# A recurrent block and a cross-attention block on one core: from one loop with both interleaved to three stages

## What is computed

```python
# layer 0, per sequence
xa = _ln(x); sx = shifted(xa) - xa
t = tanh((xa + sx * maa_x) @ maa_w1); m_j = t_j @ maa_w2        # five mixes j = w k v r g
x_j = xa + sx * (maa_j + m_j)
w = exp(-exp(time_decay + tanh(xw @ decay_w1) @ decay_w2))
r = xr @ Wr.T; k = xk @ Wk.T; v = xv @ Wv.T; g = silu(xg @ Wg.T)
# 32 heads of 16: per token   out = r . (faaaa * k v + s);  s = k v + w * s
x = x + (group_norm(out) * g) @ Wo.T
xc = _ln(x); ...; x = x + sigmoid(xr2 @ fWr.T) * (square(relu(xk2 @ fWk.T)) @ fWv.T)
# layer 1, latents = x, 16 heads of 32, keys and values from context and latents (487 rows)
q = latents @ q_w + q_b; k, v = concat(ctx, latents) @ kv_w + kv_b
attn = softmax(mask(q k / 32)); o = attn v @ out_w + out_b + latents
out = gelu(rmsnorm(o) @ mlp_w1 + mlp_b1) @ mlp_w2 + mlp_b2 + latents
```

## Time and profile before

| what | value |
|---|---|
| median of three runs | 1222.49 us |
| the profiled execution's own time | 1224.26 us |
| its span | 1222.2 us |
| mean granted clock of TensorE | 0.911 |
| first turn (no attention in it) | 0 to 151 us |
| seven turns of the loop | 151 to 1007 us, 119 to 128 us each |
| attention of the last sequence | 1007 to 1047 us |
| MLP | 1047 to 1222 us |

### The profile page before, as it was taken

How to read it: one execution, slowest core, us unless ns; L and a number is a source line. 1 busy time by engine, 2 the same in 40 slices (tenths; PEclk the granted TensorE clock), 3 DMA queues, 4 the chain that set the end, 5 groups by cost and what they waited for, 6 DMA issues and landing times.

```text
span 1222.2 us, 18100 instructions
## 1 busy us (share of the span) xinstructions
PE 1051.5 (86%) x6748; PEld 741.1 (61%) x6748; DVE 625.0 (51%) x1204; ACT 411.2 (34%) x934; POOL 270.3 (22%) x231
## 2 busy tenths in 40 slices
PE   5658998799789978997799879987998697999998
PEld 5525684368447834674477447843784364788886
DVE  2543248425952594358335842684268423644544
ACT  3112244134422442253235312442254225533332
POOL 2420143105410540144014400540053000200100
PEclk9768997899899989998899779998998895899999
DMA  7470122012201120122012201220122046000200
GB/s 286 117 225 8 33 69 67 1 48 68 66 8 40 68 66 15 33 68 66 15 33 68 66 10 38 68 66 8 40 68 66 0 182 232 1 0 0 61 0 30
DMA packets 25779, 73.23 MB, mean 60 GB/s; under 512 B 8173, under 2 KB 10093, under 8 KB 24350
## 3 DMA queue, kind: packets, MB, share of 16 engines
q1 hardware_dynamic: 25758, 72.94, 18.8%
HBM read 65.82 MB, written 7.11 MB: 60 GB/s over the span
## 4 chain that ended last, share of the span: by engine, by line
issue 41%; PE 31%; POOL 13%; DVE 7%; SPq 2%; DMA 2%; ACT 2%; POOLq 0%; DVEq 0%; ACTq 0%
POOL region L381 9%; PE bank L1241 7%; PE bank L1229 6%; PE bank L965 5%; DVE region L489 3%; PE bank L1000 3%; PE bank L972 3%; DMA region<-v_scratch 2%; PE bank L1031 2%; POOL region L384 2%; SPq L237 2%; PE bank L1015 1%; DVE region L496 1%; PE bank L1049 1%; POOL xj L374 1%
## 5 line engine op out<-in xcount | busy, mean ns | idle before, releaser
L965 PE MATMUL bank<-xj,wbig 128*128 128x112 f32 x1280 | 174.7, 302 | 29.2 <-DVE xj L533 23.8
L965 PEld LDWEIGHTS bank<-xj,wbig 128*128 128x128 f32 x1280 | 169.1, 217 | 34.2 <-DVE xj L533 25.5
L381 POOL TENSOR_TENSOR region<-region,ks 128x896 f32<-128x896 f32 x64 | 139.2, 2174 | 221.6 <-DMA region<-v_scratch 221.5
L457 DVE SCALAR_TENSOR_TENSOR tmp<-bank,vec,sx 128x112 f32<-128x112 f32 x160 | 41.7, 327 | 183.4 <-PE bank L987 181.3
L745 ACT ACTIVATE smb<-smb,nmax 112x487 f32<-112x487 f32 x128 | 88.1, 690 | 80.8 <-DVE nmax L569 80.8
L1049 PE MATMUL bank<-ident,smb 112*125 112x112 f32 (+1 forms) x512 | 88.1, 313 | 29.4 <-ACT smb L745 28.9
L496 DVE TENSOR_TENSOR region<-region,rt 128x896 f32<-128x896 f32 x64 | 105.4, 1647 | 7.4 <-ACT rt L833 1.8
L1000 PE MATMUL bank<-region,wbig 128*128 128x375 f32 x256 | 103.5, 559 | 0.0
L1015 PE MATMUL bank<-region,place 128*32 128x448 f32 x256 | 42.8, 751 | 68.7 <-DVE region L496 68.7
L1049 PEld LDWEIGHTS bank<-ident,smb 112*125 112x125 f32 (+1 forms) x512 | 66.0, 200 | 58.5 <-ACT smb L745 57.5
L569 DVE CUSTOM_DVE_ANT_0 smb<-bank,mask_b 112x487 f32<-112x487 f32 x128 | 78.1, 660 | 27.7 <-issue 27.7
(11 more groups left out here) (154 smaller groups left out, 1627.4 us busy)
## 6 DMA issues: line engine op xcount, KB each, us to landing
region<-v_scratch SPq DMA_DIRECT2D x64, 448.0 KB
wbig<-in_w SPq DMA_DIRECT2D x2, 4096.0 KB, 15.1
region<-in_ctxt SPq DMA_DIRECT2D x9, 750.0 KB, 4.6
wbig<-in_wbig SPq DMA_DIRECT2D x3, 2048.0 KB, 16.2
wbig<-in_wbig SPq DMA_DIRECT2D x3, 1024.0 KB
region<-in_wbig SPq DMA_DIRECT2D x2, 1024.0 KB, 10.9
x_in<-in_x SPq DMA_DIRECT2D x9, 224.0 KB, 2.6
v_scratch<-vt SPq DMA_DIRECT2D x32, 56.0 KB, 1.6
```

The lines of the kernel that those rows point to most:

```text
L381: g.tensor_tensor(buf, buf, ks[:, k:k + 1, 0:T].broadcast_to([P, VS, T]), ALU.mult).then_inc(s["a_ready"], 1)
L965: i = t_.matmul(tiles(dst)[:, m, :], w[:, k, m * P:(m + 1) * P], x[:, k, :], start=k == 0, stop=k == NT - 1)
```

## The change

The loop is taken apart into three stages, and all python loops over sequences are written out.

1. **Recurrent block of all sequences, a pipeline of three.** `period(i)` for i = -1 to 8 on every engine holds, interleaved in a fixed order: the scan of sequence b = i, the part behind the scan of a_ = i - 1 (group norm, Wo, channel mix), the inputs, mixes and k, v, r, g products of d = i + 1, and the last step (`latents`) of i - 2. `ks` and `gate` are double. The squares of the group norm and of the relu move from DVE to ACT. Latents go to DRAM by rows (`lat_scratch`) and by columns (`latc_scratch`).
2. **Attention of all sequences** with split products. `kv(b, n)` makes keys (n < 4) and values of all 488 rows (487 and a pad), context and latents together, in 12 fp32r products each; `query` and `output_projection` are split in three as well. `kv(b + 1, ...)` stands between the steps of `attention(b)`. ACT makes the high parts (`weight_high`, `context_high`, `attention_high`), DVE the low ones.
3. **MLP**: its 32 steps as before, its buffers elsewhere.

Each stage's buffers lie in the room of the last, in one `arena`. The core of the diff follows, engine by engine.

SP, after the stores and chunk loads of sequence 0, and at the end of stage 1:

```diff
+            def late_weights():
+                sp.dma_start(x_t[:, :], a["x"][0]).then_inc(s["xt_loaded"], 16)
...
+                        sp.dma_start(W["Wo"][p:p + HT, :, :], rows_of[j, m]).then_inc(s["wlate_loaded"], 16)
...
+                                sp.dma_start(gnv[p:p + HT, i, :], of[j, m]).then_inc(s["gnv_loaded"], 16)
+                sp.dma_start(tail[:, 1:4], a["wbig"][:, 5:8]).then_inc(s["wlate_loaded"], 16)
...
+            period(-1)
+            late_weights()
+            period(0)
+            attention_weights()
...
+            period(B)
+            wait(sp, "ffn_ready", B)
+            sp.dma_start(w1[:, :, :, :], a["w1"]).then_inc(s["w1_loaded"], 16)
+            load_context(1)
+            load_mask(0)
```

POOL, the whole of `period`:

```diff
+            def period(i):
+                a_, b, d = i - 1, i, i + 1
+                if real(d):
+                    rstd(1, d)
+                if real(b):
+                    for n in (2, 3, 4):
+                        scan_input(b, n)
+                if real(a_):
+                    rstd(2, a_)
+                if real(b):
+                    scan_input(b, 5)
+                if real(d):
+                    for j in (MIX_V, MIX_K, MIX_W):
+                        mixed(d, j)
+                if real(b):
+                    scan_input(b, 6)
+                if real(d):
+                    mixed(d, MIX_R)
+                if real(b):
+                    scan_input(b, 7)
+                if real(d):
+                    mixed(d, MIX_G)
+                    scan_input(d, 0)
+                    scan_input(d, 1)
```

ACT, in `period` and at the end of `last_period`:

```diff
+                if real(a_):
+                    deviation(a_)
+                    norm_weights(a_)
+                if real(b):
+                    gate_tanh(b)
...
+                latent_columns(a_)
+                context_high(1)
```

PE, the split products and their place between the attention's steps (groups 1 and 2 of `attention` left out):

```diff
+            def kv(b, n):
+                if n == 0:
+                    pe.wait_ge(s["cx_ready"], b + 1)
...
+                        for w, c in in_parts(parts("kw"), x):
+                            i = t_.matmul(dst[:, 0:PAD], w[:, k, n * P:(n + 1) * P], c[:, k, :],
...
+                        for w, c in in_parts(parts("vw"), x):
+                            i = t_.matmul(dst[0:KT_ROWS, :], c[:, k, r:r + KT_ROWS], w[:, k, :],
...
+            def query(b):
...
+                        for w, c in in_parts(parts("qw"), x):
+                            i = t_.matmul(tiles(7)[:, m, :], w[:, k, m * P:(m + 1) * P], c[:, k, 0:T],
...
+                scores(b, 0)
+                if more:
+                    kv(b + 1, 0)
+                probs_turned(b, 0)
+                if more:
+                    kv(b + 1, 1)
+                if b:
+                    output_projection(b - 1)
+                weighted(b, 0)
...
+                scores(b, 3)
+                if more:
+                    kv(b + 1, 6)
+                    query(b + 1)
...
+                probs_turned(b, 3)
+                if more:
+                    kv(b + 1, 7)
+                sums_turned(b)
+                weighted(b, 3)
```

More of the change, by code:

```diff
@@ new lines, in build @@
+        sx = room.take("sx", [P, NT, T])
+        t4 = room.take("t4", [P, 2, T])
+        tmp = room.take("tmp", [P, 2, NT, T])
+        xxx = tmp[:, 1]
+        xj = room.take("xj", [P, 3, NT, T])
+        dt65 = room.take("dt65", [DD + 1, T])
+        maa1 = room.take("maa1", [P, NT, NMIX * DM])
+        maa2 = room.take("maa2", [P, 2, C])
+        dec1 = room.take("dec1", [P, NT, DD])
+        dec2 = room.take("dec2", [DD + 1, C])
+        room = Room(ROOM_S, ROOM_T)
+        scan = [room.take(f"scan{i}", [P, VS, T]) for i in range(NBUF)]
@@ new lines, in build @@
+        decay = [room.take(f"decay{i}", [P, VS * T]) for i in range(2)]
+        ws = room.take("ws", [P, NT, T])
+        ks = [room.take(f"ks{i}", [P, NT, T + 1]) for i in range(2)]
+        vt = room.take("vt", [P, NT, T + 1])
+        rt = room.take("rt", [P, NT, T])
+        ruk = room.take("ruk", [P, NT, T])
+        s0 = room.take("s0", [P, NT, B, S])
+        room = Room(ROOM_T, ROOM_E)
+        x_t = room.take("x_t", [T, C])
+        x2 = room.take("x2", [T, C])
+        rows_t = room.take("rows_t", [T, C])
@@ new lines, in build @@
+        xa_t = room.take("xa_t", [P, NT, T + 1])
+        sx_t = room.take("sx_t", [P, NT, T])
+        xk = room.take("xk", [P, 2, NT, T])
+        kk = room.take("kk", [P, NT, T])
+        rr = room.take("rr", [T, C])
+        lat = room.take("lat", [T, C])
+        latc = room.take("latc", [P, NT, T])
+        y_cols = room.take("y_cols", [P, NT, T])
+        y_cen = room.take("y_cen", [P, NT, T])
+        yg = room.take("yg", [P, NT, T])
+        gstd = room.take("gstd", [P, 2, T])
+        gate = [room.take(f"gate{i}", [P, NT, T]) for i in range(2)]
@@ L210, in build, with wait, real, kv_bank @@
         s = {n: sem(n) for n in names}
+        def wait(engine, name, count):
+            if count > 0:
+                engine.wait_ge(s[name], count)
+        def real(*sequences):
+            return all(0 <= i < B for i in sequences)
+        def kv_bank(b, n):
+            return n % 2 if b == 0 else HID_BANK[n % 2]
         block = ctx.enter_context(nc.Block())
@@ new lines, in mask, with group_max @@
+            def mask(b):
+                dve.wait_ge(s[f"mask_loaded{b % 2}"], 16 * (b // 2 + 1))
+                v.tensor_scalar(mask_b[b % 2][:, T:NKEY], mask_i[b % 2][:, :], 0.0, MASKED, ALU.is_equal, ALU.mult
+                                ).then_inc(s["mask_eq"], 1)
+            def group_max(b, k, first=0, last=HG):
+                if k == 0 and first == 0:
+                    dve.wait_ge(s["mask_eq"], b + 1)
+                    dve.wait_ge(s["pad_ready"], 5)
+                dve.wait_ge(s["s_done"], b * NT + k + 1)
+                for r in range(first, last):
@@ new lines, in _, with kv_keep @@
+            for i in range(-1, B):
+                period(i)
+            def kv_keep(b, n):
+                act.wait_ge(s["kv_ready"], b * NPC + n + 1)
+                if b and n == 0:
+                    wait(act, "pvh", (b - 1) * NT)
+                src = bank[kv_bank(b, n)]
+                if n < NT:
+                    c_.activation(kt[b % 2][:, n, :], src[:, 0:NKEY], ACT.Identity,
+                                  bias=V["k_b"][:, n:n + 1]).then_inc(s["kv_kept"], 1)
+                else:
+                    c_.copy(vv[b % 2][0:KT_ROWS, n - NT, :], src[0:KT_ROWS, :]).then_inc(s["kv_kept"], 1)
@@ L924, in _ @@
+            for b in range(B):
+                attention(b)
+            act.wait_ge(s["w2_loaded"], 16)
             w2_high(0, 0)
+            attention_high(B - 1)
             def step(g, p, first=False, last=False):
```

1641 lines of the change are left out of this document (949 added, 692 removed).

## The result

Before 1226.83 us, after 1129.56 us (medians of four executions each, 1221.03 to 1233.58 and 1126.10 to 1130.95): ratio 0.920, 95% interval [0.914, 0.926]. The forecast was 1193 us with 1140 to 1256 as its range.

What follows compares the result with a forecast made beforehand. PE nearly bounds the old turn; DVE was to bound stage 1, PE stage 2. Start and period 0 to 113, middle periods and period 7 to 566, then 618, 643, attention to 1020, MLP to 1192.5: 1193 us, range 1140 to 1256.

Steps and rivals of the forecast that it cites:

- the gate's stall: Middle period: DVE's gating waits for ACT's tanh, queued behind the norm's weights; 3 us, bounds 0 and 5.
- the query at one instruction's pace: Stage 2, PE: 48 split products with 112 columns, each at half an f32 instruction's cost, 5.6 us in all.
- rival 2: Stage 2 query: split products with 112 columns cost as much as f32 ones, +45, 1238 us; chance 0.20.
- rival 3: Stage 1: DVE and POOL run almost wholly in line, a middle period of 76 us, 1258 in all; chance 0.17.
- Sum: 51 + 5 + 3 + 3.5 + 3 = 65.5, taken as 66: Middle period: DVE's work, added POOL waits, in-order stalls, seam and 0.1 us step waits; bounds 55 and 84.
- 10.6 + 5.3: DVE's attention share in the earlier turn: 16 maxima at 0.66, and smaller steps estimated at half as much.
- I take 5 more: Middle period: additional DVE waits from POOL's additions and scan inputs laid beside it; 5 us, bounds 0 and 18.
- my 6: POOL waits already in DVE's 51: products with r 4.5 us, scans about 1.5 to 2.5 per sequence.
- The seam: Between middle periods: last product with r, PE's sum, whole y, then next scan awaiting POOL's input; 3.5 us, bounds 1 and 7.
- the steps that wait for the one before: Middle period: 0.1 us between a step and one that waits for it, some 30 times; 3 us.
- Rival 4: Stage 1: periods of 60 us because POOL runs during DVE's stalls, so the two don't add; 1153 us, chance 0.18.
- 47.7 with 2 for the seam: 49.6: Stage 2, one sequence: PE's summed products 47.7 us, 2 for the seam, 49.6 in all.

Runs made afterwards that it cites:

- pool_half: Against the changed kernel, POOL multiplies only half of each chunk by the keys, leaving keys out of the other half; 1090.2 us.
- rstd_late: Against the changed kernel, POOL's small power for the first norm goes behind the multiplications of chunks 2 and 3; 1121.8 us.
- gate_first: Against the changed kernel, ACT computes the gate's tanh ahead of the group norm's weights; 1119.0 us.

## Why the prediction was wrong

- **Mechanisms.** Right: DVE sets the middle period, PE stage 2; the gate's stall (3 forecast, 3.06 measured); the query at one instruction's pace (5.6 forecast, 48 products in 5.30 measured), so rival 2 fell; DVE and POOL exclude each other without the period reaching rival 3's 76; MLP 172.5 against 173.4. PE at 1.00 in stage 2 without waiting for exps.
- **The step that failed first: "Sum: 51 + 5 + 3 + 3.5 + 3 = 65.5, taken as 66"**, measured 61.0; six of these errors are 30 of the 63 us. Its first two terms both failed. For the turn of the earlier trace rows I gave the attention 10.6 + 5.3 of DVE's 68.2 us. Its timeline shows 12.0, because the maxima follow each other more closely than they last: all 16, with their reads, are busy for 9.80. That leaves 56.2 for the recurrent block and 55 behind the two squares, not 51. Of these, 10.1 us were held already: 6.2 in the products with r, 2.4 in the scans, and 1.5 in ruk (2.60 instead of 1.07), which my 6 had left out. The maxima of that turn, and ruk in it:

```profile
397.66:516.98 119.32, 9.80 (x32) 0.94 0.15 46
```

```profile
422.12 2.60 DVE L467 SCALAR_TENSOR_TENSOR ruk<-ks,vec,rt 128x112 f32<-128x112 f32 x4
```

So "I take 5 more" for POOL was the wrong term: the pipeline holds DVE for 10.5 us, 0.4 more than that turn did (8.1 to 10.1 in six turns of the loop). pool_half and rstd_late show that the held time lies on the path, not that the change added it. The durations of all steps sum to the same (57.9 before, 57.8 after), but they follow each other more closely, and DVE is busy 53.6 us. That 51 + 5 = 56 came as near as that is luck: 4 too little and 5 too much.

- **Idle time in the period** was 7.9, not 9.5. The seam took 1.9 of its 3.5, and the steps that wait for the one before took 0.8 of their 3. Against them stand 2.2 that had no term, 1.45 of it for the Wo product. Rival 4 had the length (60 against 61.0 measured), for a reason that no run showed: it let stalls and held time overlap, and both stood in line.
- **Stage 2, "47.7 with 2 for the seam: 49.6"**, measured 46.3. PE has no seam (46.12 of 46.30 busy). The transposes were priced from one row at 1.95; from start to start four groups take 6.4, not 7.8. Scores, weighted sums and inverse sums follow each other at 1.02, 0.91 and 0.8, not at the durations 1.09, 0.98 and 0.98, 0.6 too much. The products for keys and values went the other way: 22.6 instead of 21.7, since 12 with 512 columns take 2.9 here and not the MLP's 2.77. Only the last sequence was too cheap as a whole (33, where 36.2 were measured).
- **The start, the periods 0 and 8 and the change of stages** were each 2 to 7 us too long.
- **The range.** Nearly all the terms were taken on the long side: 65.5 as 66, 5 more for POOL, 2 for a seam, 1.95 for a transpose, the late end for the fifth chunk. The bounds of one period (55 to 84) held 61, and six such periods alone could have given 66 less; yet the lower end, 1140, was taken from rival 4 alone. Errors of one sign in stages that follow each other add, and the range left no room for that.

## What to carry to other kernels

Price a dense stretch by the distance between starts of its groups, not by their durations, and put no seam into it unless an engine's row shows idle time. A path over two engines that exclude each other is shortened by laying the long instruction of one beside those that are not held; here that brought less than half of what the timeline promised, and the waits at the ring of buffers grew. Before adding waits for a second engine to a busy time, take out of it, row by row, those that it holds already. A row of small transfers and a large load are to be kept behind the transfers that a chain waits for, both at once; and a product form is to be counted with what its preparation puts on other engines: here 21 us gained, 12 lost.

## What was not expected of the hardware

- The precision form's gain turns round with the width. From start to start in stage 2, 12 split products with 512 columns take 2.88 to 2.95 us where the f32 way takes 3.53, but 48 with 112 columns take 5.30 where 32 f32 instructions take 3.56. Both short forms run at 0.11 us an instruction. A group of values of after, then the query's first product and what follows its last:

```profile
763.55 0.50 PE L1472 MATMUL bank<-vw_hi,cx_hi 128*122 128x512 f32 x1
...
766.44 0.21 PE L1487 MATMUL bank<-cx_hi,qw_hi 128*128 128x112 f32 x1
...
771.74 1.72 PE L1546 MATMUL bank<-ident,smb 112*122 112x112 f32 x16
```

- The 64 scans of DVE were seldom held (mean 2085 ns, 2.02 us alone): they mostly began first, and POOL was held in their place (3.59). A step with one wide SBUF input was held too: rows_t took 2.00 against 0.54. The Trainium skill's page SBUF — State Buffer, section Who interferes with whom, names two kinds of DVE instructions that contend with GpSimd (POOL): those with two SBUF inputs, and those in a mode that uses both ports, which it says `tensor_scalar` can enter. rows_t is a `tensor_scalar`, so its wait agrees with the page, though no run here shows the mode. Not every step with one wide input waits: in gate_first the statistics at 308.28 took their usual 0.69 us beside a POOL multiply that ran from 307.39 to 309.24.
- The Wo product, 3.60 us at the full clock, took 5.1 to 6.6 in the periods of the changed kernel. It is a PE term on DVE's path (the wait of 1.45 ahead of x). Ahead of it PE had waited 5.98, 2.02 and 0.73 us, and the granted clock was 0.50 from 239.7 to 250.0 and 0.62 up to 253.3. The longest wait alone does not decide it: in gate_first PE waited 6.82 us at the same place, but not again before the Wo product. That took 4.64 there, at a clock of 0.79, and about 3.7 in five other periods. PE in the changed kernel:

```profile
239.72 1.01 PE L1231 MATMUL bank<-ident,rows_f 112*128 112x112 f32 x4 [5.98 <-DVE rows_f L523]
...
244.41 1.72 PE L1330 MATMUL bank<-scan,place 128*32 128x448 f32 x8 [2.02 <-DVE scan L576]
...
246.86 6.46 PE L1243 MATMUL bank<-tail,yg 128*112 128x512 f32 x8 [0.73 <-DVE yg L602]
```
